# A prologue rebuilt: weights folded beside the first norm of a fused vision block

## The chip, the cores and the metric

The kernel runs on one core of a Trainium2 chip. The metric is the device time of one execution in microseconds (us), the median of several runs. The engines are TensorE (PE; its weight loads PEld), VectorE (DVE), ScalarE (ACT), GpSimd (POOL) and SyncE (SP); the last issues most of the DMA transfers, ACT issues a few at the start.

## The reference, cut to what matters

Four images are cut into patches and embedded; a class token goes ahead of them (3137 tokens of 128 features each). A gated delta attention and then a feed-forward block with mixed expert weights follow.

```python
emb = jnp.einsum('blk,ek->ble', patches, W) + b            # K = 48 pixels
x0  = jnp.concatenate([cls_tok, emb], axis=1)
xn  = _layernorm(x0)
q_c = _dwconv_causal(_linear(xn, Wq, bq), cwq, cbq)         # 4 taps; the same for k and v
...
outs = scan(gated delta rule over q, k, v with gates from Wa, Wb)
h1  = x0 + (gated, normalised outs) @ Wo.T + bo
y   = h1 + layernorm(hn + FFN(hn)), with FFN weights mixed by a gate of hn
```

(The snippet is shortened from the reference, whose parts are nested functions. `hn` is the normalised `h1`.)

## The kernel before, in words

The tokens go through in 25 steps of 128 tokens, each for the four images at once. A software pipeline of five stages runs over the steps: the body for index `j` does the embedding stage E of step `j+2`, the projections F of step `j+1`, the inner triangular solve I of step `j`, the state update C of step `j-1` and the output stage H of step `j-2`. The first body is `j = -2` (`first`) and has only stage E of step 0. Each engine runs its own program of these bodies in an order written out by hand, and semaphores tie the engines together; an engine runs its instructions strictly in that order. After the last body the feed-forward part begins, 25 units of it.

Because the embedding is linear, the kernel never forms q, k and v from the normalised tokens by two products. It folds, once, in the prologue: the embedding weights `We` (48 pixel rows, a bias row, an empty row and a class row, `KX` = 51 in all) are centred (`Wc`, the mean over the 128 features taken off), transposed (`WcT`), multiplied with all projections (`rhs_all`: k, v, gate, q and the two scalar gates, 514 columns) and, for k, v and q, multiplied with the four convolution taps. The taps are spread over partitions by small products with selection matrices (`selA`, `selB`, `cwT`), and the convolution's bias by one with `onehot1` and `cb_row`. The results are `SA` and `SB`. From then on a step's projections are products of `SA` and `SB` with `xs`, the pixel columns times the norm's reciprocal deviation.

That deviation takes a trip: stage E multiplies pixels and `We` (L1088), DVE takes the statistics (L810, L818), POOL the power -1/2 (L625, L628), PE transposes the four columns to rows (L1111), ACT copies them to SBUF (L479), SP writes them to HBM (L395), waits, and reads them back broadcast over partitions (L400, L401). DVE multiplies them with the pixels to `xs` (L911), ACT copies the shifted half (L528), and then PE may start the projections of the step (L1050, L1051), the first thing of the body `j = -1` on it.

In the body `j = -2` DVE runs `fold_weights` and `sub_masks` (L711 to L725) ahead of L911; PE runs its `fold_weights` at the very end of the body. All eight early weight loads share one semaphore, `w_in`, and the bias row `bo_rows` for the residual shares `we_in` with the embedding's weights. In `fold_weights` DVE makes every step wait for the one before (`step_done`). `apart(engine)` issues a no-operation between a wait and the next instruction.

The scalar program begins so:

```python
for s in (0, 1):
    act.dma_start(xt[s][0:KX], x[:, :, s * C:(s + 1) * C]).then_inc(xt_in[s], 16)
for dst, src in weights_early[1::2]:
    act.dma_start(dst, src).then_inc(w_in, 16)
```

## Time and profile before

| | before |
|---|---|
| median of 3 runs | 891.03 us (890.76 to 892.22) |
| profiled execution, its own time | 895.05 us |
| its span in the profile | 893.2 us |
| PE busy | 838.4 us (94%) |
| DVE busy | 664.9 us (74%) |
| ACT busy | 482.1 us (54%) |
| POOL busy | 355.4 us (40%) |

A span is what the profiler saw from the first to the last instruction; the execution's own time has 1.85 us more around it. Busy time counts matmuls from start to modelled end, and since they overlap in a pipeline a busy PE is not one at its peak. Times of rows are microseconds from the span's start.

### The profile page before, as it was taken

To read this page: it belongs to the slowest core of one execution; us is meant where nothing else is said; L and a number is where in the kernel's file an instruction comes from. 1 tells how busy PE (TensorE), PEld (TensorE's weight loads), DVE (VectorE), ACT (ScalarE), POOL (GpSimd) and SP (SyncE) were. 2 spreads that over 40 slices of the span, in tenths; PEclk is the share of its full clock that TensorE was granted. 3 is DMA by queue.
4 is the path that set the end of the run, shared out by engine and by line. 5 is a ranking of instruction groups with operands and counts; after the bars stand their busy time and mean duration, and the time that the engine had idled before them with its cause. 6 is when DMAs were issued, how large, how long until landed. Compare 5 with 4: busy or idle time off the path is not lost. (4 is left out here: it accounts for less than half of the span.)

```text
span 893.2 us, 31060 instructions
## 1 busy us (share of the span) xinstructions
PE 838.4 (94%) x11766; PEld 634.7 (71%) x11766; DVE 664.9 (74%) x2420; ACT 482.1 (54%) x1721; POOL 355.4 (40%) x530
## 2 busy tenths in 40 slices
PE   5689999999999999999999999999985999999996
PEld 2357777777777777777777777777764677777775
DVE  3466888888888888888888888888764676868434
ACT  0434455565655565565655565566523355666654
POOL 3122333233332332233332332333211178888875
PEclk9999999999999999999999999999958799999999
DMA  2000121222111110111110110111100233333431
GB/s 62 10 13 12 48 54 49 59 60 59 38 53 48 36 32 24 36 36 37 32 35 24 33 34 24 37 31 30 28 26 24 90 96 111 107 107 114 122 119 43
DMA packets 78659, 45.33 MB, mean 51 GB/s; under 512 B 20357, under 2 KB 69803, under 8 KB 78511
## 3 DMA queue, kind: packets, MB, share of 16 engines
q1 hardware_dynamic: 77663, 42.80, 16.8%
q8 instruction: 95, 1.56, 0.7%
q10 hardware_dynamic: 848, 0.54, 0.2%
q14 instruction: 53, 0.43, 0.2%
HBM read 23.69 MB, written 19.63 MB: 49 GB/s over the span
## 5 line engine op out<-in xcount | busy, mean ns | idle before, releaser
L1050 PE MATMUL bank<-SA,work 128*128 128x386 f32 x200 | 93.5, 550 | 6.5 <-ACT work L528 6.5
L1647 PEld LDWEIGHTS bank<-work 128*128 128x128 f32 x768 | 89.6, 192 | 12.5 <-issue 12.5
L1529 ACT ACTIVATE work<-bank,b1mix 128x512 f32<-128x512 f32 x96 | 66.0, 687 | 59.4 <-PE bank L1621 59.3
L438 ACT ACTIVATE logit<-bank 128x2 f32<-128x2 f32 x100 | 17.3, 173 | 149.3 <-PE bank L1051 149.1
L1647 PE MATMUL bank<-work 128*128 128x128 f32 x768 | 89.9, 275 | 0.8 <-DVE work L1407 0.8
L616 POOL TENSOR_SCALAR var2e<-mv 128x4 f32<-128x4 f32 x25 | 5.7, 227 | 211.1 <-DVE mv L795 211.1
L1621 PE MATMUL bank<-work 128*128 128x512 f32 x192 | 86.5, 593 | 0.0
L1051 PE MATMUL bank<-SB,work 128*128 128x256 f32 x200 | 60.8, 386 | 0.0
L1621 PEld LDWEIGHTS bank<-work 128*128 128x128 f32 x192 | 34.6, 190 | 34.6 <-issue 34.4
L1010 PEld LDWEIGHTS bank<-work 32*32 32x32 f32 x3200 | 35.6, 108 | 32.9 <-issue 27.2
L1051 PEld LDWEIGHTS bank<-SB,work 128*128 128x128 f32 x200 | 38.9, 194 | 27.9 <-issue 1.8
L1446 DVE TENSOR_TENSOR work<-bank,work 128x512 f32<-128x512 f32 x24 | 16.6, 691 | 56.1 <-PE bank L1647 56.1
L1010 PE MATMUL bank<-work 32*32 32x32 f32 x3200 | 46.1, 195 | 8.9 <-DVE work L950 8.0
L1038 PEld LDWEIGHTS bank<-work 32*32 32x32 f32 x3200 | 35.1, 108 | 26.6 <-issue 21.1
L639 POOL COPY work<-work 32x128 f32<-32x128 f32 x50 | 14.1, 282 | 94.9 <-DVE work L755 93.8
L1038 PE MATMUL bank<-work 32*32 32x32 f32 x3200 | 46.1, 195 | 4.0 <-DVE work L744 4.0
L753 DVE TENSOR_TENSOR work<-bank,work 128x128 f32<-128x128 f32 x100 | 28.6, 286 | 27.6 <-PE bank L1038 27.5
L486 ACT ACTIVATE work<-bank 128x128 f32<-128x128 f32 x100 | 26.2, 277 | 41.5 <-PE bank L1125 41.5
L441 ACT ACTIVATE work<-bank 128x384 f32<-128x384 f32 x100 | 48.5, 485 | 0.0
L744 DVE TENSOR_TENSOR work<-bank,masks 128x128 f32<-128x128 f32 x100 | 28.5, 285 | 26.5 <-PE bank L1010 26.3
L625 POOL TENSOR_SCALAR var1e<-mv 128x4 f32<-128x4 f32 x25 | 5.6, 224 | 100.5 <-DVE mv L818 100.5
L634 POOL TENSOR_TENSOR expo<-euler,logit 128x8 f32<-128x8 f32 x25 | 40.9, 1636 | 6.8 <-ACT logit L438 4.0
(233 smaller groups left out, 2287.8 us busy)
## 6 DMA issues: line engine op xcount, KB each, us to landing
hn_kept<-work SPq DMA_DIRECT2D x25, 256.0 KB, 2.3
hnT_kept<-work SPq DMA_DIRECT2D x25, 256.0 KB, 2.3
work<-hnT_kept SPq DMA_DIRECT2D x25, 256.0 KB, 2.9
work<-hn_kept SPq DMA_DIRECT2D x25, 256.0 KB, 3.1
out_dram<-work SPq DMA_DIRECT2D x24, 256.0 KB, 2.5
tv<-in_L_ffn_tv_W_dram SPq DMA_DIRECT2D x16, 256.0 KB
work<-r_kept SPq DMA_DIRECT2D x25, 98.0 KB
work<-in_x_dram SPq DMA_DIRECT2D x23, 102.0 KB
```

Source lines behind the costliest of these rows:

```text
L441: nc.scalar.activation(kvg[s % 3][:, b, :], bank[4 - b % 2][:, 0:384], ACT.Silu).then_inc(kvg_ready, 1)
L486: ins = nc.scalar.activation(sq_q[:, b, :], by4(bank[1])[:, b, :], ACT.Square, accum_out=ssq[:, b:b + 1])
L634: nc.gpsimd.tensor_tensor(expo[:, :], euler[:, :], logit[:, :], ALU.pow).then_inc(expo_ready, 1)
L744: nc.vector.tensor_tensor(newblk[k], by32(blk_ps), masks32[:, MASKED.index(k), :].unsqueeze(1).broadcast_to([D, NB, SUB]), ALU.mult).then_ ...
L753: nc.vector.tensor_tensor(Xd[par], by32(X_ps), Xd[par], ALU.add).then_inc(X_ready, 1)
L1010: ins = mm(by32(blk_ps)[sub(r), b], Bm[par][sub(r), b, sub(r)], Yd[par][sub(r), b, :], start=True, stop=True)
L1038: ins = mm(by32(X_ps)[sub(r), b], newblk[k][sub(r), b, :], Xd[par][sub(r), b, :], start=True, stop=True)
L1050: mm(t[:, 0:386], xs[p][:, b, HIST:XW], SA[:, 0:386], start=True, stop=False)
L1051: mm(t[:, 0:256], xs[p][:, b, 1:1 + C], SB[:, 0:256], start=False, stop=True).then_inc(kvg_ps, 1)
L1529: ins = nc.scalar.activation(hid[f][:, :], ps[:, :], ACT.Relu, bias=b1mix[:, of[0], f:f + 1])
L1621: ins = mm(ps[:, :], w1T[of[0]][:, f, :], ghT[par][:, :, :].rearrange("p t c -> p (t c)"), start=True, stop=True)
L1647: ins = mm(by4(bank[2 + par])[:, t, :], hid[f][:, t * C:(t + 1) * C], w2T[of[t]][:, f, :], start=(f == 0 and t == 0), stop=(f == FB - 1), ...
```

## The change

It touches the prologue above all. The weight loads get semaphores of their own: `taps_in` for the taps, `proj_in` for the projections and their biases, `bo_in` for the residual's bias row, `w_in` for what is needed later; they are issued in another order. PE first runs eight products of `ones` with itself whose result nobody reads (`WARM`), then the three products of taps and convolution bias, then stage E of step 0, and its `fold_weights` stands right behind that instead of at the end of the body, ahead of L1111. The product with the projections is cut into two parts, k, v and q first and the gates behind them, so 514 columns are made in four pieces instead of two. ACT keeps the three results of the taps in SBUF and the gate part of `SA`; it runs one Silu on ones before that. DVE centres the weights before the statistics, copies `WcT` right behind them, and multiplies the taps straight out of PSUM with six operations, with no copy to `fold`; the chain `step_done` is gone. `h` of step 0 is kept behind the copy of `WcT`. Elsewhere two `apart(dve)` of stage E go, and the last feed-forward unit counts on the semaphores of the other units instead of its own.

```diff
@@ -338,13 +347,12 @@
             return not isinstance(j, int) or 0 <= j + lag < STEPS
 
         first, last = -2, STEPS + 1
+        WARM = 8
 
         def iterations(body):
             for j in range(first, last + 1):
                 body(j, j % 2)
 
-        DVE_PRO = 16
-
         LE, LF, LI, LC, LH = 2, 1, 0, -1, -2
         TV_FROM = 2
         block = ctx.enter_context(nc.Block())
@@ -357,14 +365,13 @@
 
         embedding = [
             (We[0:PIX, :], tok_WT[:, :]), (We[PIX:PIX + 1, :], row1(tok_b)),
-            (We[PIX + 2:PIX + 3, :], tok_cls.rearrange("a b p -> (a b) p")), (bo_rows[:, :], bo.partition_broadcast(D)),
+            (We[PIX + 2:PIX + 3, :], tok_cls.rearrange("a b p -> (a b) p")),
         ]
-        weights_early = [
-            (cwT, taps_kvq[:, :]), (bias_row[:, 0:514], row1(biases[0:514])), (cb_row[:, 0:384], row1(biases[514:898])),
-            (rhs_all[:, 0:514], projections[:, :]), (nat[:, 0, :], WoT[:, :]), (nat[:, 1, :], gfc1_wT[:, :]),
-            (nw_col, col1(norm_w)), (gfc1_bc[:, :], col1(gfc1_b)),
-        ]
-        W_IN = 16 * len(weights_early)
+        conv_taps = [(cwT, taps_kvq[:, :]), (cb_row[:, 0:384], row1(biases[514:898]))]
+        projection = [(rhs_all[:, 0:514], projections[:, :]), (bias_row[:, 0:514], row1(biases[0:514]))]
+        later_sp = [(nat[:, 0, :], WoT[:, :]), (nw_col, col1(norm_w))]
+        later_act = [(nat[:, 1, :], gfc1_wT[:, :]), (gfc1_bc[:, :], col1(gfc1_b))]
+        W_IN = 16 * (len(later_sp) + len(later_act))
 
 
         ffn = make_ffn(nc, ctx, sb, sem, work, locals())
@@ -374,7 +381,10 @@
             sp.wait_ge(We_zero, 1)
             for dst, src in embedding:
                 sp.dma_start(dst, src).then_inc(we_in, 16)
-            for dst, src in weights_early[0::2]:
+            for dst, src in conv_taps:
+                sp.dma_start(dst, src).then_inc(taps_in, 16)
+            sp.dma_start(bo_rows[:, :], bo.partition_broadcast(D)).then_inc(bo_in, 16)
+            for dst, src in later_sp:
                 sp.dma_start(dst, src).then_inc(w_in, 16)
             ffn["load"](sp)
 
@@ -419,10 +429,21 @@
         @block.scalar
         def _(act):
 
-            for s in (0, 1):
-                act.dma_start(xt[s][0:KX], x[:, :, s * C:(s + 1) * C]).then_inc(xt_in[s], 16)
-            for dst, src in weights_early[1::2]:
+            act.dma_start(xt[0][0:KX], x[:, :, 0:C]).then_inc(xt_in[0], 16)
+            for dst, src in projection:
+                act.dma_start(dst, src).then_inc(proj_in, 16)
+            act.dma_start(xt[1][0:KX], x[:, :, C:2 * C]).then_inc(xt_in[1], 16)
+            for dst, src in later_act:
                 act.dma_start(dst, src).then_inc(w_in, 16)
+            act.wait_ge(ones_set, 1)
+            nc.scalar.activation(gate_sums[:, 0, :], ones[:, 0:NB], ACT.Silu)
+            act.wait_ge(taps_ps, 1)
+            for t, i in ((cwA, 0), (cwB, 4), (cbs, 2)):
+                ins = nc.scalar.copy(t, bank[i][:, 0:384])
+            ins.then_inc(taps_kept, 1)
+            act.wait_ge(gate_ps, 1)
+            nc.scalar.copy(SA[0:64, 256:386], bank[6][0:64, 0:130]).then_inc(gate_kept, 1)
+
             def body(j, par):
                 p = 1 - par
 
@@ -660,19 +681,12 @@
 
         @block.vector
         def _(dve):
-            done = [0]
-
-            def step_done(ins):
-
-                done[0] += 1
-                ins.then_inc(pro_dve, 1)
-                dve.wait_ge(pro_dve, done[0])
-
             nc.vector.memset(We[:, :], 0.0).then_inc(We_zero, 1)
             ffn["vector_early"](dve)
 
             nc.vector.memset(Wc, 0.0)
             nc.vector.memset(WcT, 0.0)
+            nc.vector.memset(SA[64:128, 256:386], 0.0)
             nc.vector.memset(xs[0], 0.0)
             nc.vector.memset(xs[1], 0.0)
             for t in X:
@@ -680,38 +694,42 @@
             nc.vector.memset(Y, 0.0)
             nc.vector.memset(state, 0.0).then_inc(zeroed, 1)
 
+            def center_weights():
+                dve.wait_ge(we_in, 16 * len(embedding))
+                dve.wait_ge(zeroed, 1)
+                nc.vector.tensor_reduce(wsum[0:KX, :], We[0:KX, :], AX.X, ALU.add).then_inc(pro_dve, 1)
+                dve.wait_ge(pro_dve, 1)
+                nc.vector.tensor_scalar(wmean[0:KX, :], wsum[0:KX, :], 1.0 / D, None, ALU.mult).then_inc(pro_dve, 1)
+                dve.wait_ge(pro_dve, 2)
+                nc.vector.tensor_scalar(Wc[0:KX, :], We[0:KX, :], wmean[0:KX, :], None, ALU.subtract).then_inc(Wc_ready, 1)
+
             def fold_weights():
+                dve.wait_ge(WcT_ps, 1)
+                nc.vector.tensor_copy(WcT.rearrange("p (h c) -> p h c", h=2)[:, :, 0:KX],
+                                      bank[3][:, 0:KX].unsqueeze(1).broadcast_to([D, 2, KX])).then_inc(WcT_ready, 1)
+
+            def fold_taps():
+                dve.wait_ge(fold_ps, 1)
+                dve.wait_ge(taps_kept, 1)
+                kv, q = bank[5][:, 0:256], bank[5][:, 256:384]
+                nc.vector.tensor_tensor(SA[:, 0:256], cwA[:, 0:256], kv, ALU.mult).then_inc(pro_dve, 1)
+                nc.vector.tensor_tensor(SA[:, 386:514], cwA[:, 256:384], q, ALU.mult).then_inc(pro_dve, 1)
+                dve.wait_ge(pro_dve, 3)
+                nc.vector.tensor_tensor(SA[:, 0:256], cbs[:, 0:256], SA[:, 0:256], ALU.add)
+                nc.vector.tensor_tensor(SB[:, 0:256], cwB[:, 0:256], kv, ALU.mult)
+                dve.wait_ge(pro_dve, 4)
+                nc.vector.tensor_tensor(SA[:, 386:514], cbs[:, 256:384], SA[:, 386:514], ALU.add)
+                nc.vector.tensor_tensor(SB[:, 384:512], cwB[:, 256:384], q, ALU.mult).then_inc(folded, 1)
+
+            def output_weights():
                 dve.wait_ge(con, 2)
-                dve.wait_ge(zeroed, 1)
-                step_done(nc.vector.tensor_reduce(ident32[:, :], ident[:, :].rearrange("p (r c) -> p c r", r=SUBS), AX.X, ALU.add))
+                nc.vector.tensor_reduce(ident32[:, :], ident[:, :].rearrange("p (r c) -> p c r", r=SUBS), AX.X, ALU.add).then_inc(pro_dve, 1)
+                dve.wait_ge(w_in, W_IN)
+                nc.vector.tensor_scalar(Wo_T[:, :], nat[:, 0, :], nw_col, None, ALU.mult)
+                nc.vector.tensor_copy(gfc1_T[:, :], nat[:, 1, :])
+                dve.wait_ge(pro_dve, 5)
                 for t in Xd:
                     nc.vector.tensor_copy(t, ident32[:, :].unsqueeze(1).broadcast_to([D, NB, SUB]))
-
-                dve.wait_ge(we_in, 16 * len(embedding))
-                dve.wait_ge(w_in, W_IN)
-                step_done(nc.vector.tensor_reduce(wsum[0:KX, :], We[0:KX, :], AX.X, ALU.add))
-                step_done(nc.vector.tensor_scalar(wmean[0:KX, :], wsum[0:KX, :], 1.0 / D, None, ALU.mult))
-                step_done(nc.vector.tensor_scalar(Wc[0:KX, :], We[0:KX, :], wmean[0:KX, :], None, ALU.subtract))
-                step_done(nc.vector.tensor_scalar(Wo_T[:, :], nat[:, 0, :], nw_col, None, ALU.mult))
-                step_done(nc.vector.tensor_copy(gfc1_T[:, :], nat[:, 1, :]))
-
-                dve.wait_ge(pro_pe, 1)
-                step_done(nc.vector.tensor_copy(WcT.rearrange("p (h c) -> p h c", h=2)[:, :, 0:KX],
-                                                bank[3][:, 0:KX].unsqueeze(1).broadcast_to([D, 2, KX])))
-                dve.wait_ge(pro_pe, 2)
-                step_done(nc.vector.tensor_copy(fold[:, 0:512], bank[5][:, :]))
-                step_done(nc.vector.tensor_copy(fold[:, 512:514], bank[6][:, 0:2]))
-                for dst, taps in ((SA, bank[0]), (SB, bank[4])):
-                    step_done(nc.vector.tensor_tensor(dst[:, 0:256], taps[:, 0:256], fold[:, 0:256], ALU.mult))
-                    dst_q = dst[:, 386:514] if dst is SA else dst[:, 384:512]
-                    step_done(nc.vector.tensor_tensor(dst_q, taps[:, 256:384], fold[:, 384:512], ALU.mult))
-                step_done(nc.vector.tensor_tensor(SA[:, 0:256], bank[2][:, 0:256], SA[:, 0:256], ALU.add))
-                step_done(nc.vector.tensor_tensor(SA[:, 386:514], bank[2][:, 256:384], SA[:, 386:514], ALU.add))
-
-                nc.vector.memset(SA[64:128, 256:386], 0.0)
-                nc.vector.tensor_copy(SA[0:64, 256:384], fold[0:64, 256:384])
-                step_done(nc.vector.tensor_copy(SA[0:64, 384:386], fold[0:64, 512:514]))
-                assert done[0] == DVE_PRO
 
             def sub_masks():
 
@@ -801,22 +819,34 @@
                     need(dve, vmean_ready, s)
                     nc.vector.tensor_reduce(vsum[:, :], kvg[s % 3][:, :, D:2 * D], AX.X, ALU.add).then_inc(vsum_ready, 1)
                 grow(2)
+                if j == first:
+                    center_weights()
                 if on(j, LE):
                     s = j + LE
+
+                    def keep_h0():
+                        if s == 0:
+                            dve.wait_ge(bo_in, 16)
+                        h = h1buf[:, :, bass.ds(s, 1), :].rearrange("p b s c -> p b (s c)")
+                        nc.vector.tensor_tensor(h, by4(bank[1]), bo_rows[:, :].unsqueeze(1).broadcast_to([D, NB, D]), ALU.add).then_inc(h0_kept, 1)
+
                     dve.wait_ge(h0_ps, s + 1)
                     need(dve, mv1_ready, s)
-                    apart(dve)
                     for b in range(NB):
                         ins = nc.vector.bn_stats(stats1[:, b, :], by4(bank[1])[:, b, :])
                     ins.then_inc(stats1_done, 1)
-                    h = h1buf[:, :, bass.ds(s, 1), :].rearrange("p b s c -> p b (s c)")
-                    nc.vector.tensor_tensor(h, by4(bank[1]), bo_rows[:, :].unsqueeze(1).broadcast_to([D, NB, D]), ALU.add).then_inc(h0_kept, 1)
+                    if s > 0:
+                        keep_h0()
                     dve.wait_ge(stats1_done, s + 1)
                     need(dve, var1e_ready, s)
-                    apart(dve)
                     for b in range(NB):
                         ins = nc.vector.bn_aggr(mv1[:, b, :], stats1[:, b, :])
                     ins.then_inc(mv1_ready, 1)
+                    if s == 0:
+                        fold_weights()
+                        keep_h0()
+                        fold_taps()
+                        output_weights()
                 new_blocks(3)
                 if on(j, LH):
                     s = j + LH
@@ -899,8 +929,7 @@
                     dve.wait_ge(rk2_ready, s + 1)
                     need(dve, cdecay_ready, s)
                     nc.vector.scalar_tensor_tensor(cneg[:, :], rk2[:, :], -1.0, ab[:, 4:8], ALU.mult, ALU.mult).then_inc(cneg_ready, 1)
-                if isinstance(j, int) and j == first:
-                    fold_weights()
+                if j == first:
                     sub_masks()
                 if on(j, LE):
                     s = j + LE
@@ -961,26 +990,30 @@
         def _(pe):
             mm = nc.tensor.matmul
             tr = nc.tensor.transpose
+            pe.wait_ge(ones_set, 1)
+            for i in range(WARM):
+                mm(bank[7][:, 0:D], ones[:, :], ones[:, :], start=True, stop=True)
             pe.wait_ge(con, 2)
+            pe.wait_ge(taps_in, 16 * len(conv_taps))
+            mm(bank[0][:, 0:384], selA, cwT, start=True, stop=True)
+            mm(bank[4][:, 0:384], selB, cwT, start=True, stop=True)
+            mm(bank[2][:, 0:384], onehot1, cb_row[:, 0:384], start=True, stop=True).then_inc(taps_ps, 1)
             pe.wait_ge(we_in, 16 * len(embedding))
-            pe.wait_ge(zeroed, 1)
 
             def fold_weights():
-                pe.wait_ge(w_in, W_IN)
-
-                mm(bank[0][:, 0:384], selA, cwT, start=True, stop=True)
-                mm(bank[4][:, 0:384], selB, cwT, start=True, stop=True)
-                mm(bank[2][:, 0:384], onehot1, cb_row[:, 0:384], start=True, stop=True)
-                pe.wait_ge(pro_dve, 4)
-                tr(bank[3][:, 0:D], Wc, ident[:, :]).then_inc(pro_pe, 1)
-                pe.wait_ge(pro_dve, 7)
-
-                mm(bank[5][:, :], WcT, rhs_all[:, 0:512], start=True, stop=False)
-                mm(bank[5][:, :], onehot2, bias_row[:, 0:512], start=False, stop=True)
-                mm(bank[6][:, 0:2], WcT, rhs_all[:, 512:514], start=True, stop=False)
-                mm(bank[6][:, 0:2], onehot2, bias_row[:, 512:514], start=False, stop=True).then_inc(pro_pe, 1)
-                pe.wait_ge(pro_dve, DVE_PRO)
-                pe.wait_ge(con, 2 + 2 * len(MASKED))
+                pe.wait_ge(zeroed, 1)
+                pe.wait_ge(Wc_ready, 1)
+                tr(bank[3][:, 0:D], Wc, ident[:, :]).then_inc(WcT_ps, 1)
+                pe.wait_ge(WcT_ready, 1)
+                pe.wait_ge(proj_in, 16 * len(projection))
+                for to, at, n in ((0, 0, 256), (256, 384, 128)):
+                    mm(bank[5][:, to:to + n], WcT, rhs_all[:, at:at + n], start=True, stop=False)
+                    ins = mm(bank[5][:, to:to + n], onehot2, bias_row[:, at:at + n], start=False, stop=True)
+                ins.then_inc(fold_ps, 1)
+                for to, at, n in ((0, 256, 128), (128, 512, 2)):
+                    mm(bank[6][:, to:to + n], WcT, rhs_all[:, at:at + n], start=True, stop=False)
+                    ins = mm(bank[6][:, to:to + n], onehot2, bias_row[:, at:at + n], start=False, stop=True)
+                ins.then_inc(gate_ps, 1)
 
             def body(j, par):
                 p = 1 - par
@@ -1087,6 +1120,8 @@
                     for b in range(NB):
                         ins = mm(by4(bank[1])[:, b, :], xt[par][0:KX, b, :], We[0:KX, :], start=True, stop=True)
                     ins.then_inc(h0_ps, 1)
+                if j == first:
+                    fold_weights()
                 level_update(2)
                 if F_:
                     pe.wait_ge(kvg_ready, NB * s1 + 1)
@@ -1173,8 +1208,10 @@
                         pe.wait_ge(og_ready, NB * c + b + 1)
                         ins = tr(by4(bank[7])[:, b, :], og[:, b, :], ident[:, :])
                     ins.then_inc(ogT_ps, 1)
-                if isinstance(j, int) and j == first:
-                    fold_weights()
+                if j == first:
+                    pe.wait_ge(taps_kept, 1)
+                    pe.wait_ge(folded, 1)
+                    pe.wait_ge(gate_kept, 1)
 
             iterations(body)
             ffn["tensor"](pe)
...
@@ -1466,25 +1497,25 @@
-                                    fhnb[par][:, ts, :], ALU.add).then_inc(last_res, 1)
-            dve.wait_ge(last_res, i + 1)
+                                    fhnb[par][:, ts, :], ALU.add).then_inc(res_ready, 1)
+            dve.wait_ge(res_ready, LASTU + i + 1)
...
```

## Rows read from the trace of the kernel before

**Rows 1.** Waits, all engines, 0 to 30 us: total, times, longest.

```profile
ACT work L528 <- DVE work L911: 15.5, 1, 15.5
```

**Rows 2.** Waits of PE, 130 to 680 us: total, times, longest.

```profile
PE bank L1010 <- DVE work L950: 4.0, 20, 0.2
```

**Rows 3.** Timeline of the start: start, duration, engine, line, operands, count, idle before.

```profile
0.79 0.20 POOL L552 MEMSET ones<- 128x128 f32 x1 [0.29 <-POOLq L1681]
...
2.30 0.37 SPq L376 DMA_DIRECT2D bo_rows<-in_L_attn_bo_dram  x1
...
3.08 0.52 SPq L378 DMA_DIRECT2D work<-in_biases_dram  x1
...
6.07 2.04 PE L1088 MATMUL bank<-We,work 51*128 51x128 f32 x8 [6.07 <-DMA bo_rows<-in_L_attn_bo_dram]
...
8.23 0.89 DVE L810 BATCH_NORM_STATS2 stats<-bank 128x6 f32<-128x128 f32 x4 [3.61 <-PE bank L1088]
...
9.63 0.37 DVE L818 BATCH_NORM_AGGREGATE mv<-stats 128x2 f32<-128x6 f32 x4
...
10.67 0.28 DVE L692 TENSOR_REDUCE work<-We 51x1 f32<-51x128 f32 x1
...
11.60 0.37 PE L1111 MATMUL bank<-ident,rstd 128*4 128x128 f32 x1 [3.49 <-POOL rstd L628]
...
12.29 0.25 SPq L395 DMA_DIRECT2D r_kept<-work  x1
...
13.77 0.26 SPq L401 DMA_DIRECT2D work<-r_kept  x1
```

**Rows 4.** Timeline of the fold, to the first projections.

```profile
11.90 1.64 PE L971 MATMUL bank<-work 4*128 4x384 f32 x2
...
16.04 0.47 PE L975 MATMUL bank<-ident,work 128*128 128x128 f32 x1
16.62 0.26 DVE L699 COPY work<-bank 128x102 f32<-128x102 f32 x1 [4.25 <-PE bank L975]
...
16.94 2.08 PE L978 MATMUL bank<-work 128*128 128x512 f32 x2 [0.42 <-DVE work L699]
...
20.95 0.59 PE L980 MATMUL bank<-work 128*128 128x2 f32 x2
...
23.07 0.42 DVE L705 TENSOR_TENSOR SA<-bank,work 128x256 f32<-128x256 f32 x1
...
25.09 0.29 DVE L709 TENSOR_TENSOR SA<-bank,SA 128x128 f32<-128x128 f32 x1
...
26.04 0.17 DVE L719 MEMSET masks<- 128x128 f32 x1
...
27.03 0.68 DVE L911 TENSOR_TENSOR work<-work 51x512 f32<-51x512 f32 x1
...
28.57 1.63 PE L1050 MATMUL bank<-SA,work 128*128 128x386 f32 x2 [6.53 <-ACT work L528]
```

**Rows 5.** Busy time of DVE in one short stretch: stretch, length, busy (count), PEclk, DMA.

```profile
11.45:12.40 0.95, 0.86 (x2) 1.00 0.00 0
```

**Rows 6.** Timeline, rows of the next body.

```profile
33.05 1.16 PE L1088 MATMUL bank<-We,work 51*128 51x128 f32 x8
...
40.74 0.26 SPq L401 DMA_DIRECT2D work<-r_kept  x1
...
42.36 1.06 PE L1159 MATMUL bank<-work 128*128 128x128 f32 x8
...
42.71 0.69 DVE L911 TENSOR_TENSOR work<-work 51x512 f32<-51x512 f32 x1
```

**Rows 7.** Busy time of PE and its granted clock (the column after the count).

```profile
28.00:33.00 5.00, 4.43 (x8) 1.00 0.08 21
46.50:47.00 0.50, 0.50 (x32) 0.57 0.08 26
49.50:50.00 0.50, 0.50 (x33) 0.51 0.00 0
```

43 lines of the change are left out of this document (23 added, 20 removed).

## Prediction

> **What bounds the kernel now.** I read the waits of PE in the steady part first: the largest comes once a step, 0.2 us behind the small transpose of DVE [rows 2]. PE and DVE pace the loop, and the change does nothing there. So its worth lies ahead of the first projections. The waits of the first 30 us show ACT waiting 15.5 us for the product that makes `xs` [rows 1]; the timeline says why. The norm's trip is early: L401 is issued at 13.77 us [rows 3], and the same transfer lets L911 run 1.97 us after its issue one step later (40.74 to 42.71, where DVE had ended its work 0.1 us before) [rows 6], so the row was there by 15.7. L911 starts only at 27.03, because DVE must first end `fold_weights` and `sub_masks` [rows 4]. The fold ends last, with 11.3 us of slack beside it. 1.54 us after L911 PE starts L1050 [rows 4]; everything later hangs on that start through semaphores alone, no timer and no late load, so I carry a shift of L911 to the end one to one.
>
> **A note on PE's clock.** The granted clock reads 1.00 over the first 33 us [rows 7], yet stage E's eight matmul records take 2.04 us at 6.07 and 1.16 at 33.05 [rows 3, 6]. By durations PE is on the low of its two levels (1.2 GHz) until about 33, then on the high one (2.4). Dense work began at 28.57 and the high rate was there 4.5 us later; it began near 46.5 and the clock rose at 50.0, 3.5 us later [rows 4, 6, 7]. Between 11.90 and 22 PE was nearly always busy and stayed low (L978 2.08 us) [rows 4], largely with products that use one or four rows. It fell at about 46.6, 3.1 us after its last dense work ended at 43.42 [rows 6, 7].
>
> **The change, part by part.** Let H be the end of stage E's product, 8.11 before.
>
> *Warm matmuls.* Stage E's four products took 2.04 us, 0.51 each [rows 3], so eight take 4.1 at the low rate, from 1.0 (`ones` is set then [rows 3]) to 5.1. They cost nothing while the taps are still on their way; without that cover, up to 4.1.
>
> *Loads.* The taps move ahead of `bo_rows`, so their last part is issued near 2.7 instead of 3.08 [rows 3]. Landing isn't shown. From L395 to L401 are 1.48 us with a small transfer's whole way in them, and `bo_rows`, issued at 2.30, released PE at 6.07, 3.8 later [rows 3]. By these the taps land between 4.2 and 6.5; I take 5.5, nearer to the neighbour in the same queue. The only hard upper bound is that `w_in` was full when L692 began at 10.67. The projections and the bias on ACT's queue are issued earlier than before and needed later than 11; free. `bo_in` is waited for behind the copy of `WcT`, past 10: free; were it late, the taps' six operations would queue behind it.
>
> *The taps' products first.* From L971 to L975 they took 4.14 us [rows 4]; they now stand ahead of stage E. At the low rate: 5.5 + 4.1 + 2.04, H = 11.7. At the high rate half of that, by the two times of stage E [rows 3, 6]: 5.5 + 2.2 + 1.16, H = 8.9. If the clock rises at the end of the warm matmuls and falls some 3 us later, near 8, the taps run mostly high (2.6) and stage E low: H = 10.1. That is what I take, since 4.1 us of dense work lies between the 3.5 and 4.5 that two rises took.
>
> *Beside the first norm.* The centring (L692 to L694, 0.78 from 10.67 to the stretch at 11.45 [rows 3, 5]) goes in front of the statistics, into DVE's wait. L813, the 0.5 between L810 and L818, goes behind [rows 3]. `WcT` is copied at H + 1.5 (0.12 + 0.89 + 0.37 and gaps) for 0.26; its transpose (0.47) hides under the statistics. PE folds from H + 1.85. Two passes of 512 columns take about 2.0 [rows 4]; k, v and q are 384 columns in two contributions: 3.0 at the low rate. The gates: 128 columns in two contributions, 1.0, and the two scalar columns twice 0.55 (L980) [rows 4], 2.1. So k, v, q end at H + 4.85, the gates at H + 6.95. The three copies of taps on ACT (some 0.6 each, by DVE's 0.42 for 256 columns [rows 4]) have the 4 us and more between the taps' end and that moment.
>
> *DVE behind the fold.* The six operations from L705 to L709 took 2.31 us (23.07 to 25.38) [rows 4]; the new six have the same shapes: H + 7.25. Gone are 1.0 for the copies to `fold` (L980 and its equal L981 end near 22.05, L705 starts at 23.07) and 0.66 for three small operations (25.38 to 26.04). `output_weights` takes the 0.7 between L818's end and L692 [rows 3] and the 0.86 of Wo and gfc1 [rows 5]: H + 8.9. `sub_masks`, 0.99 (26.04 to 27.03) [rows 4]: DVE is free at H + 9.9. POOL makes the masks that it waits for behind its power, from H + 3.0 on; they have 5.9 us, and no row shows how much of it they need.
>
> *The norm's trip is now behind the fold.* L1111 queues behind the gates' products on PE, and L479 behind `gate_kept` on ACT; the reciprocal deviation is ready at H + 3.0 (11.60 less 8.11, less the 0.5 of L813). From L1111 to SP's L395 are 0.69, to L401 another 1.48 [rows 3], to L911 1.97 [rows 6]: H + 6.95 + 4.15 = H + 11.1. It ends 1.2 after DVE. So the wait moves from the fold to the row's transfer, which had been hidden; if that landed 1.2 sooner, DVE would be next.
>
> The Trainium skill ("DMA: Bandwidth & Descriptors", Anatomy of one DMA) puts a fixed cost of about 2.0 us on every DMA, mostly the receipt. The first of the two transfers here needs less than that by the rows; an estimate by the page would make the trip some 0.8 longer.
>
> *Rest.* ACT's second table load goes with the early Silu; the two `apart` stand where DVE waits for PE anyway; the merged semaphores keep every wait. All nothing.
>
> **Sum.** L911 at 10.1 + 11.1 = 21.2 instead of 27.03: 5.8 us earlier. The profiled execution's 895.05 (span 893.2 and 1.85 around it) would be 889.2. It lies 4.0 above the median of the runs shown, so the shift is taken off that: 891.03 - 5.8 = 885.2. The clock's later rises may fall otherwise by one us either way; with the taps' landing that gives the forecast's own range, 884.0 to 886.4.
>
> **Rivals.**
> *The clock never rises in the prologue.* The second rise took 3.5 us, the first 4.5, so 4.1 may be too few; the low-row products behind did not lift it before. H = 11.7, L911 at 22.8, 4.2 gained: 886.8.
> *It stays high through the fold.* H = 8.9; k, v, q 1.5; the gates 1.05; DVE is free at H + 8.3 and the row there at H + 8.5. L911 at 17.4, 9.6 gained: 881.4. Against it: from 5.1 on PE has only thin products and gaps, and it fell 3.1 us after dense work ended. In between (high for stage E too) 7 gained: 884.0.
> The Trainium skill ("TensorE: Matmul & The Clock Gate", Part 1) states that the low rate is the default, that sustained activity lifts it and idleness drops it again. By that rule the first rival is a matter of how the eight matmuls fall in time, run by run, and the second unlikely. The trace agrees in both rises and the fall named above.
> *The taps land late.* PE is in order: stage E, once at 6.07, stands behind them. The only hard bound is 10.67. Landing then gives H = 10.6 + 4.1 + 2.04 = 16.7, L911 at 27.8: 0.8 slower, 891.8. It decides from a landing at 9.8. For it: `w_in`'s larger loads fill the same queues at that time. Against: the taps are a few KB ahead of them in the queue, and PE was released by the fourth load at 6.07.
> *The gain is given back.* If something later ran on its own clock (loads, the clock's phases), the end would stay: 891.0. Against it: the waits show none of that kind [rows 1, 2].
>
> **How the numbers follow.** Forecast 0.45, clock never up 0.22, higher clock for longer 0.2 (half of it within 884), taps late 0.06, given back 0.07. Faster, same, slower by 0.2% (1.8 us, about what a measurement can tell from no change): the first three cases give 0.87, the lost gain and half of the late taps fall within, 0.10, and the other half, with a landing still later than the old order's bound, gives 0.03. The range reaches down to 882.6, leaving out the fully high clock, and up to 887.8, past the clock that never rises with the taps a microsecond late.
>
> **What would show it.** Stage E's records ending near 10 and lasting 2.04 (or 1.16: then higher); the taps' products in 2.6; the product to `xs` starting near 21, DVE idle before it by about 1 us with a DMA as releaser; PE's first projections near 22.8; the distance from there to the span's end unchanged within 1.5 us. The forecast is wrong if stage E comes later than 12, if a load holds PE past 7, or if DVE, not the row, ends last.

## The result, and the profile after

The changed kernel takes 889.08 us (median of 20 runs, 886.18 to 892.96); the kernel before, run beside it, 892.56 (20 runs). The ratio is 0.9965, with a 95% interval of 0.9953 to 0.9977: 3.1 us faster, 2.1 to 4.2. The forecast was 885.2 with a range of 882.6 to 887.8 and a gain of 5.8 us, so the time lies above the range and the gain is 3.1 of the 5.8. 1.5 us of the miss in absolute time is the reference: the three runs shown before had a median of 891.03. The rest is a real shortfall.

The profiled execution took 890.64 us, its span is 888.8. PE in the prologue, to the first product that uses the finished row, by the timeline:

```profile
1.05 3.79 PE L995 MATMUL bank<-ones 128*128 128x128 f32 x16 [1.05 <-POOL ones L573]
6.42 1.61 PE L998 MATMUL bank<-work 4*128 4x384 f32 x2 [1.59 <-DMA work<-in_biases_dram]
...
10.52 2.07 PE L1121 MATMUL bank<-We,work 51*128 51x128 f32 x8
12.53 0.47 PE L1006 MATMUL bank<-ident,work 128*128 128x128 f32 x1
14.14 1.22 PE L1010 MATMUL bank<-work 128*128 128x256 f32 x2 [1.14 <-DVE work L708]
15.29 1.22 PE L1011 MATMUL bank<-work 1*128 1x256 f32 x2
16.43 0.80 PE L1010 MATMUL bank<-work 128*128 128x128 f32 x2
...
17.88 0.80 PE L1014 MATMUL bank<-work 128*128 128x128 f32 x2
...
19.33 0.59 PE L1014 MATMUL bank<-work 128*128 128x2 f32 x2
...
20.36 0.38 PE L1146 MATMUL bank<-ident,rstd 128*4 128x128 f32 x1
```

The warm matmuls (L995) are over at 4.84. PE then stands idle 1.6 us for the last load of the taps, at work from 6.42, and stage E (L1121) comes at 10.52 where it came at 6.07 before [rows 3]. It takes 2.07 us, against 2.04 before and 1.16 at the high clock [rows 6]: the clock has not risen. The transpose of the reciprocal deviation (L1146) stands behind all four pieces of the fold.

The same execution on the other engines:

```profile
12.63 0.89 DVE L836 BATCH_NORM_STATS2 stats<-bank 128x6 f32<-128x128 f32 x4 [6.27 <-PE bank L1121]
...
17.99 0.42 DVE L715 TENSOR_TENSOR SA<-work,bank 128x256 f32<-128x256 f32 x1 [3.31 <-PE bank L1011]
...
19.39 0.28 DVE L722 TENSOR_TENSOR SB<-work,bank 128x128 f32<-128x128 f32 x1
...
20.73 0.76 DVE L741 TENSOR_REDUCE masks<-masks 128x16 f32<-128x64 f32 x4
...
21.05 0.25 SPq L405 DMA_DIRECT2D r_kept<-work  x1
22.22 0.27 SPq L410 DMA_DIRECT2D work<-r_kept  x1
22.53 0.26 SPq L411 DMA_DIRECT2D work<-r_kept  x1
24.34 0.68 DVE L940 TENSOR_TENSOR work<-work 51x512 f32<-51x512 f32 x1 [2.85 <-issue]
```

DVE has ended everything else at 21.49 and idles 2.85 us ahead of L940, the product to `xs`. Its releaser is not shown, but between the read's issue at 22.53 and 24.34 nothing else is under way that L940 waits for: it is the row's transfer. L940 starts 2.69 us earlier than L911 did [rows 4].

From there on nothing has changed but the clock's phases. Starts of the product to `xs` of the first and the last step, of the sum over the gates (the first instruction of the feed-forward part on DVE), and the span, for the profiled execution of every kernel of this study whose profile is used:

```
kernel              first xs  last xs   gate sum  span    xs to xs  xs to sum  sum to end
before              27.03     618.11    696.56    893.2   591.08    78.45      196.64
changed             24.34     615.59    691.99    888.8   591.25    76.40      196.81
changed again       25.04     617.92    696.38    893.1   592.88    78.46      196.72
no warm             24.45     616.07    687.92    884.5   591.62    71.85      196.58
row first           22.15     616.64    690.43    887.3   594.49    73.79      196.87
norm first          18.41     610.32    686.25    883.0   591.91    75.93      196.75
... and no warm     19.67     611.06    686.94    883.5   591.39    75.88      196.56
... and warm 12     17.75     608.30    684.23    881.0   590.55    75.93      196.77
one product         23.34     614.63    691.03    887.8   591.29    76.40      196.77
masks early         17.73     609.00    684.89    881.7   591.27    75.89      196.81
tap loads first     19.93     613.08    689.01    885.9   593.15    75.93      196.89
changed, warm 12    22.93     613.86    692.36    889.0   590.93    78.50      196.64
best again          16.55     611.37    685.21    882.0   594.82    73.84      196.79
```

The feed-forward part is the same to 0.3 us. The loop differs by up to 4.3 us and the stretch from the last `xs` to the gate sum by up to 6.7, and much of that is chance between executions: the changed kernel and its repetition differ by 4.3 us in span with 0.7 of it at the first `xs`. So a single span says little here, the start of the first `xs` says what the prologue did, and the median of many runs says what it is worth. Where the 6.7 us come from the granted clock shows. For the changed kernel, then for the one with no warm matmuls, PE's busy time and granted clock (the column after the count):

```profile
650.00:660.00 10.00, 8.18 (x186) 0.56 0.09 29
...
680.00:690.00 10.00, 3.73 (x14) 0.64 0.13 42
690.00:700.00 10.00, 10.00 (x35) 0.50 0.36 118
```

```profile
650.00:660.00 10.00, 7.08 (x230) 1.00 0.10 30
...
680.00:690.00 10.00, 6.63 (x21) 0.51 0.38 116
```

In the pipeline's last bodies PE has gaps. In the first execution the clock is at its low level (1.2 GHz) for more than half of the 50 us from 650, in the second it stays high (2.4 GHz) until after 680. All thirteen profiles fall in line: over the stretch from the last `xs` to the gate sum the mean granted clock is 0.82 in the three that take 78.5 us, 0.85 in the seven that take 75.9 to 76.4, 0.89 in the two that take 73.8, and 0.95 in the one that takes 71.85. The 890.64 of the changed kernel's profile against the 895.05 before holds 2.7 us of the change and 1.7 of this kind.

### The profile page after: what moved, and what is told of

The parts are those of the page before. It is cut to its first block and busy times, and to the rows that moved or that the text cites. A ratio compares the mean times of both kernels' runs of the same rounds, so it can differ in the third digit from the quotient of the medians.

```text
span 888.8 us, 31105 instructions
## 1 busy us (share of the span) xinstructions
PE 841.8 (95%) x11790; PEld 639.4 (72%) x11790; DVE 663.8 (75%) x2416; ACT 482.7 (54%) x1725; POOL 356.1 (40%) x530
```

## The experiments

Except where it says otherwise each kernel is the changed kernel with the edit shown. Ratios are to the kernel before, run on the same chip, with their 95% interval.

**The changed kernel again.** 

> The changed kernel once more, unaltered, as the measure for the other runs of this chip. In its first profile the eight warm matmuls ran at the low clock to their end (3.79 us from 1.05), stage E ended at 12.59 us and the product to xs began at 24.34. Theory A (the warm matmuls rarely or never raise the clock): this profile shows the same three numbers within 0.3 us, and the time is 3 to 4 us below the kernel before. Rival B (they raise it in some executions): with luck this profile shows stage E in some 1.2 us instead of 2.07 and the product to xs before 22.5; the median is the same, since it mixes both.

No edit. Median 888.56 us (12 runs), ratio 0.9962 (0.9946 to 0.9979). The low clock again (3.79 us for the warm matmuls, 2.07 for stage E); the taps landed later, at 6.80, and `xs` started at 25.04, 0.7 later than in the first profile, of which 0.4 is the landing and 0.3 the row's read. That is outside the 0.3 of theory A; for the clock theory A stands by this one profile, but it can't tell how often the clock rises.

**No warm matmuls.** 

> The changed kernel with none of the eight warm matmuls. Theory A (they do nothing but run under the taps' loads): the taps' products start at 6.4 as before, stage E ends at 12.6, the product to xs starts at 24.3, and the time equals the changed kernel's within 0.5 us. Rival B (in some executions they raise the clock, which is where the 0.8 us of median gain beyond the 2.7 us of the profile's prologue come from): the median is 0.8 to 1.5 us above the changed kernel's.

```diff
-        WARM = 8
+        WARM = 0
```

Median 889.78 us, ratio 0.9962 (0.9944 to 0.998): the same ratio as with the eight. The taps' products start at 6.50, `xs` at 24.45. The eight have cost nothing, and no gain of theirs can be told in the time.

**The row's transpose ahead of the gates.** 

> The changed kernel, but the transpose of the reciprocal deviation stands on PE between the products of k, v, q and those of the gates, and ACT copies the row before the gate columns. Theory A (the row's trip behind the gates' products is now what ends last): the row starts at 18.0 instead of 20.4, its trip of 4.0 us ends at 22.0, DVE is free at 21.5; the product to xs starts near 22.0, 2.3 us earlier, and the time falls by 2.3. Rival B (DVE's chain or the later bodies take it back): the product to xs moves by less than 0.5 us, or it moves and the end does not.

```diff
                 ins.then_inc(fold_ps, 1)
+
+            def fold_gates():
                 for to, at, n in ((0, 256, 128), (128, 512, 2)):
...
                     tr(bank[7][0:NB, 0:C], rstd1[:, :], ident[:, :]).then_inc(r_row_ps, 1)
+                if j == first:
+                    fold_gates()
...
-            act.wait_ge(gate_ps, 1)
-            nc.scalar.copy(SA[0:64, 256:386], bank[6][0:64, 0:130]).then_inc(gate_kept, 1)
...
                     nc.scalar.copy(rrows[64:64 + NB, 0, :], bank[7][0:NB, 0:C]).then_inc(r_row_ready, 1)
+                    if s == 0:
+                        act.wait_ge(gate_ps, 1)
+                        nc.scalar.copy(SA[0:64, 256:386], bank[6][0:64, 0:130]).then_inc(gate_kept, 1)
```

`xs` starts at 22.15, 2.2 us earlier than in the changed kernel's profile. The median is 885.52, 3.0 below the changed kernel on the same chip, the ratio 0.9943 (0.9921 to 0.9965); the two intervals overlap, so the move of `xs` is the better evidence. The row and DVE are now nearly level:

```profile
20.32 0.26 SPq L411 DMA_DIRECT2D work<-r_kept  x1
...
21.00 0.76 DVE L742 TENSOR_REDUCE masks<-masks 128x16 f32<-128x64 f32 x4
22.15 0.68 DVE L941 TENSOR_TENSOR work<-work 51x512 f32<-51x512 f32 x1 [0.40 <-DVE masks L742]
```

DVE's idle time has shrunk from 2.85 us to 0.40, and 1.83 us again lie between the read's issue and `xs`. The row's trip behind the gates' products was what ended last in the changed kernel; here it and DVE's chain end within half a microsecond.

**Stage E ahead of the taps' products.** 

> As the run before it, and besides the taps' products stand behind stage E and the transpose of the centred weights instead of ahead of them, and the row's transpose ahead of the products of k, v, q. Theory A (the wait for the taps' loads, then their 4.1 us, delays stage E and the whole fold): stage E starts at 5.5 to 6.1 instead of 10.5, the taps run under DVE's statistics and the power, k, v, q start near 12.6 instead of 14.1, the row lands by 17, and DVE's chain ends last near 20.2: 4.1 us earlier than the changed kernel, 6.8 before the kernel before. Rival B (the order of the two does not matter, since PE has the same sum of work before the fold): the product to xs starts no earlier than in the run before it, near 22.0.

Beside the edit of the run before (the transposes of the later steps stay where they were; the guards for that are left out here):

```diff
             pe.wait_ge(con, 2)
-            pe.wait_ge(taps_in, 16 * len(conv_taps))
-            mm(bank[0][:, 0:384], selA, cwT, start=True, stop=True)
-            mm(bank[4][:, 0:384], selB, cwT, start=True, stop=True)
-            mm(bank[2][:, 0:384], onehot1, cb_row[:, 0:384], start=True, stop=True).then_inc(taps_ps, 1)
             pe.wait_ge(we_in, 16 * len(embedding))
...
                 tr(bank[3][:, 0:D], Wc, ident[:, :]).then_inc(WcT_ps, 1)
+                pe.wait_ge(taps_in, 16 * len(conv_taps))
+                mm(bank[0][:, 0:384], selA, cwT, start=True, stop=True)
+                mm(bank[4][:, 0:384], selB, cwT, start=True, stop=True)
+                mm(bank[2][:, 0:384], onehot1, cb_row[:, 0:384], start=True, stop=True).then_inc(taps_ps, 1)
+                pe.wait_ge(rstd1_ready, 1)
+                tr(bank[7][0:NB, 0:C], rstd1[:, :], ident[:, :]).then_inc(r_row_ps, 1)
                 pe.wait_ge(WcT_ready, 1)
```

Median 884.79 us, ratio 0.9919 (0.989 to 0.9948). `xs` starts at 18.41, 1.8 us earlier than expected. In this execution eight warm matmuls did raise the clock (stage E 1.13 us, the first of the taps' products 1.13 for 1.64 [rows 4]). The clock is taken out by the next run; without it `xs` is still 0.5 us ahead of the expectation.

**That, without warm matmuls.** 

> The kernel that puts stage E and the row's transpose ahead (the run of that name: product to xs at 18.41 us, stage E in 1.13 us at the high clock) without the eight warm matmuls. Theory A (its gain is mostly the order; the clock that rose in that one execution gave it stage E and one pass of the taps' products at the high rate): stage E takes 2.04 us from 6.1, the product to xs starts 1.3 to 1.6 us later, at 19.7 to 20.0. Rival B (the order is worth little and the raised clock made most of it): the product to xs starts after 21.5.

```diff
-        WARM = 8
+        WARM = 0
```

Median 885.13 us, ratio 0.9908 (0.9887 to 0.9928). Stage E takes 2.04 us from 5.77, and `xs` starts at 19.67: 1.3 us later than with the raised clock and 4.7 earlier than in the changed kernel. The order is worth these 4.7, 2.2 of them the row's place and 2.5 stage E's (good to 0.3, since the taps landed 0.3 us later in the profile that gives the split). The raised clock is worth 1.3, which the two ratios are too wide to show.

**That, with twelve.** 

> The same kernel with twelve warm matmuls, 5.7 us at the low clock, up to 6.7. Theory A (eight are too few in most executions, twelve are enough in nearly all): this profile shows stage E in some 1.15 us and the product to xs at 18.4 to 19.0; if the clock rises the twelve end before 6.1 and cost nothing. Rival B (no number of matmuls on constants raises it reliably): stage E takes 2.04 us and starts at 6.7, the product to xs at 20.5, and the time is 0.5 us above the run with none.

```diff
-        WARM = 8
+        WARM = 12
```

```profile
1.05 5.23 PE L996 MATMUL bank<-ones 128*128 128x128 f32 x24 [1.05 <-POOL ones L574]
6.21 1.16 PE L1126 MATMUL bank<-We,work 51*128 51x128 f32 x8
...
8.31 0.80 PE L1006 MATMUL bank<-work 4*128 4x384 f32 x2
8.95 1.15 PE L1007 MATMUL bank<-work 1*128 1x384 f32 x2
```

At the low rate a further record of this shape adds 0.21 us, so 24 would take 5.49 by the 3.79 for 16; they took 5.23, so the clock rose among the last of them. Stage E is short, a pass of the taps' products costs 0.80 a pair, and the last pair spans the fall. `xs` starts at 17.75, earlier than the 18.4 to 19.0 expected. Median 882.98 us, ratio 0.989 (0.9871 to 0.9909).

**One product instead of the cut one.** 

> The changed kernel with the product of weights and projections in the two pieces of the kernel before (512 and 2 columns) instead of four; the gate columns are copied by ACT only when DVE has ended the fold, since both sit in one PSUM bank. Theory A (each piece costs a fixed 0.3 us per contribution beside its columns, so the cut costs 1.1 us on the path that ends last, the row's trip behind the gates): the products end 5.1 us after they start instead of 6.2, and the product to xs starts 1.1 earlier, near 23.2, although the fold on DVE starts 0.3 later. Rival B (the extra is not the cut but the bank or the rows of the operands): the products take 6.2 us again and the product to xs stays at 24.3.

```diff
-                for to, at, n in ((0, 0, 256), (256, 384, 128)):
...
+                mm(bank[5][:, :], WcT, rhs_all[:, 0:512], start=True, stop=False)
+                mm(bank[5][:, :], onehot2, bias_row[:, 0:512], start=False, stop=True).then_inc(fold_ps, 1)
-                for to, at, n in ((0, 256, 128), (128, 512, 2)):
+                for to, at, n in ((0, 512, 2),):
```

ACT copies the row first, then waits for DVE's `folded` and copies the gate columns from the two banks; DVE reads q at columns 384 to 512.

```profile
14.29 2.07 PE L1012 MATMUL bank<-work 128*128 128x512 f32 x2 [1.13 <-DVE work L711]
16.29 2.07 PE L1013 MATMUL bank<-work 1*128 1x512 f32 x2
18.29 0.59 PE L1015 MATMUL bank<-work 128*128 128x2 f32 x2
...
19.33 0.37 PE L1147 MATMUL bank<-ident,rstd 128*4 128x128 f32 x1
```

From the first product to the row's transpose 5.04 us instead of 6.22, and `xs` starts at 23.34, 1.0 us earlier. Median 889.85 us, ratio 0.9956 (0.9936 to 0.9975); the time alone would not tell it from the changed kernel. A pair of records costs 2.0 us for 512 columns, 1.15 for 256 and 0.73 for 128: between these 0.3 us and 3.3 ns a column (a pair of 2 columns costs 0.52). The cut buys DVE 0.25 us of start and costs the row 1.2.

**Output weights and masks before the fold.** 

> The kernel with stage E ahead (eight warm matmuls), and besides DVE makes the output weights and the small masks while it waits for the products of k, v, q, ahead of the fold with the taps. Theory A (DVE's chain ends last there: it was idle 5.6 us before the fold and then did 1.9 us of work that nothing in the fold needs): the product to xs starts when the fold ends and the row has landed, 1.7 us earlier than in that run, 16.7 with a raised clock and 18.2 without; 8 to 10 us below the kernel before. Rival B (POOL's masks are late, or the row's trip is the next bound within 0.5 us): it moves by less than 0.7 us.

Added to the kernel with stage E ahead, with eight warm matmuls (`sub_masks` leaves its old place, and the counts waited for on `pro_dve` follow the new order):

```diff
-                        fold_taps()
                         output_weights()
+                        sub_masks()
+                        fold_taps()
```

Median 883.64 us, ratio 0.9895 (0.9875 to 0.9916). The clock had not risen in the profile. `xs` starts at 17.73, 1.9 us earlier than at the same clock with no warm matmuls. PE's first projections came 1.86 us behind it, where it had been 1.5: ACT copies the gate columns in between.

**All of it.** 

> All that helped so far: stage E and the row's transpose ahead, output weights and masks made while DVE waits, and twelve warm matmuls. Theory A (each removes its own piece): stage E in 1.16 us from 6.2, the fold on DVE from 14.2, the product to xs near 15.9 to 16.0, the first projections near 17.8, 10 to 11 us ahead of the kernel before, and the median 10 us below it. Rival B (the copy of the gate columns on ACT, behind the gates' products, holds the shifted copy of xs and PE): the first projections start later than 18.2 although the product to xs is at 16.

Added to the kernel of the run before:

```diff
-        WARM = 8
+        WARM = 12
```

One of its five executions, the profiled one, took 1570 us. The median of the five is 882.64 us, of the other four 882.59, and the ratio of these 0.9876 (0.9853 to 0.9899). In the profile of the long one PE alone is slow: it is busy for 1540.9 us, by 841.3 in the repetition below, while DVE is busy for 671.9, by 663.6. A record of 386 columns (L1087) takes 930 ns on average, where in the repetition it takes 899 while the clock is low and 540 in the middle of the loop. Why PE ran at no more than its low rate all through isn't known. The kernel was therefore run once more.

**The taps' loads issued first.** 

> The changed kernel with the two loads of taps and convolution bias issued ahead of the three of the embedding instead of behind them, so the second is issued at 1.5 us instead of 2.6. Theory A (a load lands some 3.8 us behind its issue and the taps' landing at 6.4 starts the whole chain): the taps' products start near 5.3, stage E ends near 11.5, the product to xs starts 1.1 us earlier, near 23.2. Rival B (they land by how full the queues are, not by when they are issued, or the embedding's weights become late): they start after 6.0 and the product to xs moves by less than 0.4 us.

```diff
+            for dst, src in conv_taps:
+                sp.dma_start(dst, src).then_inc(taps_in, 16)
             for dst, src in embedding:
                 sp.dma_start(dst, src).then_inc(we_in, 16)
-            for dst, src in conv_taps:
-                sp.dma_start(dst, src).then_inc(taps_in, 16)
```

```profile
1.05 3.58 PE L995 MATMUL bank<-ones 128*128 128x128 f32 x16 [1.05 <-POOL ones L573]
...
1.51 0.23 SPq L383 DMA_DIRECT2D work<-in_biases_dram  x1
...
4.71 0.91 PE L998 MATMUL bank<-work 4*128 4x384 f32 x2
...
6.84 1.33 PE L1121 MATMUL bank<-We,work 51*128 51x128 f32 x8
...
19.93 0.68 DVE L940 TENSOR_TENSOR work<-work 51x512 f32<-51x512 f32 x1 [2.87 <-issue]
```

The taps' products follow the warm matmuls without an idle time, so the load issued at 1.51 was there by 4.71, within 3.2 us; issued at 2.61 it had been there at 6.42. The clock had risen here too, so the 4.4 us at `xs` are not all the loads': 1.7 by the earlier start, 2.0 by the taps' products (2.1 us instead of 4.1), 0.7 by stage E. The earlier start is worth more than the 1.1 expected. It could not come much sooner, since POOL finishes the last of the selection matrices (L598) at 4.65. Median 887.12 us, ratio 0.9931 (0.991 to 0.9953).

**The changed kernel with twelve.** 

> The changed kernel with twelve warm matmuls instead of eight. Theory A (the prediction's central case, a raised clock that falls some 3 us later, was right in its mechanism and failed since eight matmuls do not raise the clock): the taps' products take 2.7 to 2.9 us instead of 4.1, stage E ends near 11.3 instead of 12.6, and the product to xs starts near 23.0. Rival B (the thin products of the taps are no faster at the raised clock, or it falls before them): they take 4.1 us and the product to xs stays within 0.3 us of 24.3.

```diff
-        WARM = 8
+        WARM = 12
```

```profile
1.05 4.71 PE L995 MATMUL bank<-ones 128*128 128x128 f32 x24 [1.05 <-POOL ones L573]
6.47 0.88 PE L998 MATMUL bank<-work 4*128 4x384 f32 x2 [0.71 <-DMA work<-in_biases_dram]
7.19 0.80 PE L999 MATMUL bank<-work 4*128 4x384 f32 x2
7.84 1.12 PE L1000 MATMUL bank<-work 1*128 1x384 f32 x2
8.89 2.07 PE L1121 MATMUL bank<-We,work 51*128 51x128 f32 x8
```

This is the case that the prediction took for the likeliest: the taps at the raised clock (2.4 us), the fall ahead of stage E, stage E low. It ends at 10.96 and `xs` starts at 22.93, by 23.0 expected. The 24 records took 4.71 us, 0.8 less than the 5.49 of the low rate. Median 887.54 us, ratio 0.9933 (0.9908 to 0.9957), whose interval overlaps that of the changed kernel.

**All of it, again.** 

> The kernel with all that helped, unaltered, for a profile of a usual execution. Theory A: as expected of it before, stage E in 1.16 us from 6.2, the product to xs near 16.0, the median 10 us below the kernel before. Rival B (ACT's copy of the gate columns, which waits for the gates' products on PE to end near 16.7, holds the shifted copy of xs that stands behind it): the product to xs starts near 16.0 but the first projections start 1.9 us behind it instead of 1.5.

No edit to the kernel with all of it. Median 882.07 us, ratio 0.9872 (0.9854 to 0.989): 11.4 us below the kernel before, the fastest of the study. On DVE, ACT and PE:

```profile
1.05 5.49 PE L995 MATMUL bank<-ones 128*128 128x128 f32 x24 [1.05 <-POOL ones L574]
6.46 1.44 PE L1125 MATMUL bank<-We,work 51*128 51x128 f32 x8
...
10.96 0.37 PE L1008 MATMUL bank<-ident,rstd 128*4 128x128 f32 x1 [0.67 <-POOL rstd L650]
...
16.55 0.68 DVE L940 TENSOR_TENSOR work<-work 51x512 f32<-51x512 f32 x1
16.74 0.58 PE L1019 MATMUL bank<-work 1*128 1x2 f32 x2
17.25 0.90 SPq L395 DMA_DIRECT2D work<-in_x_dram  x1
17.37 0.26 ACT L501 COPY SA<-bank 64x130 f32<-64x130 f32 x1 [5.51 <-PE bank L1019]
17.65 0.62 ACT L550 COPY work<-work 51x520 f32<-51x520 f32 x1
18.42 1.62 PE L1087 MATMUL bank<-SA,work 128*128 128x386 f32 x2 [1.09 <-ACT work L550]
```

`xs` starts 0.5 us later than expected. The twelve took 5.49 us, the low rate to their end, and the clock rose only among stage E's records, which took 1.44 us, between the 1.16 of the high and the 2.07 of the low clock; stage E so ended 0.5 us later than in the run with twelve above (7.90 and 7.37). Rival B is right beside theory A: the copy of the gate columns waits for the gates' products, the shifted copy of `xs` (L550) stands behind it, and the first projections start 1.87 us after `xs`. Besides, PE idles 0.67 us ahead of the row's transpose (L1008) for POOL's power, with the products of k, v, q queued behind. Neither was tried.

Set side by side, the gain at the first `xs` of the one profile (27.03 less its start) and the gain by the ratio (of some 893.5 us):

| kernel | gain at `xs`, us | gain by the ratio, us |
|---|---|---|
| changed | 2.7 | 3.1 |
| changed again | 2.0 | 3.4 |
| no warm | 2.6 | 3.4 |
| row first | 4.9 | 5.1 |
| norm first | 8.6 | 7.2 |
| norm first, no warm | 7.4 | 8.2 |
| norm first, twelve | 9.3 | 9.8 |
| one product | 3.7 | 3.9 |
| masks early | 9.3 | 9.4 |
| tap loads first | 7.1 | 6.2 |
| changed, twelve | 4.1 | 6.0 |
| best again | 10.5 | 11.4 |

They run together within 2 us, about the uncertainty of the ratios.

## Why the prediction was wrong, point by point

**What bounds the kernel.** Right. The prologue's chain to `xs` goes one to one into the time, within the 2 us that can be told, by all the kernels set side by side above. The two `apart` and the merged semaphores were priced at nothing and not tried alone; the loop (591.08 and 591.25 us from first to last `xs`) and the feed-forward part (196.64 and 196.81) give them no room.

**Warm matmuls.** The step that failed: "That is what I take", the clock that rises at the end of the warm matmuls, and with it H = 10.1 (H is the end of stage E's product). The clock stayed low and H was 12.59. Of seven used profiles with eight warm matmuls (changed, again, row first, norm first, one product, masks early, tap loads first) the clock rose in two, so the first rival, 4.2 us gained, was the likelier case. What a raised clock does was priced rightly: with twelve, in the changed kernel, the central case came out as described (stage E's end at 10.96, `xs` at 22.93). Whether it rises in time was luck. With twelve it rose in all three profiles, but by the records' durations some eight records before their end in one (4.71 us, which is about where eight matmuls end), among the last few in another (5.23), and behind their end in the third (5.49). So eight fell short, and twelve are not sure either. The prediction gave the wrong one of the two cases more than double the other's chance, from two rises that took 3.5 and 4.5 us of dense work, with 4.1 in hand (3.79 as it turned out, less than that).
The Trainium skill ("TensorE: Matmul & The Clock Gate", Part 1) warns that the point of the rise varies from run to run of one kernel. The traces agree: after eight warm matmuls the clock stayed low in five executions and rose in two, and after twelve it rose at three different points.

**Loads of the taps.** 5.5 was taken, 6.42 came, at the upper end of the 4.2 to 6.5 named, and 6.80 in the repetition, past it. 0.9 us. The nearer neighbour was `bo_rows` with 3.8 from issue to use; the taps' last load took the same 3.8 (2.61 to 6.42), and 4.2 in the repetition. The small write of the row was no measure for a read at the start.

**The taps' products first.** 4.1 at the low rate, right. That they stand ahead of stage E was priced, and seen as the change's cost; the runs with the order turned show that cost at some 2.5 us of `xs`.

**The fold.** Priced by columns, 5.1 us for k, v, q and gates; it took 6.2. A pair of records has a fixed share of 0.3 us beside its columns, and the change makes eight pairs out of four. The run with one product gave back 1.0 at `xs`. This is the second step that failed.

**DVE.** Six operations were to take 2.31 and took 1.68. Each is about as long as before (0.42 and 0.28 us, by 0.42 and 0.29), though one side now comes from SBUF; what is gone are the waits of each for its neighbour, so they overlap. DVE was free at H + 8.9, by H + 9.9 expected.

**The row's trip as the new end.** Right: L1146 to L940 took 3.98, against 4.14, with DVE idle before; the 1.97 taken for the read was an upper bound, since DVE had been at work until 0.1 us before, and the read took 1.81. `xs` came at H + 11.75 instead of H + 11.1, the excess from the fold.

**The sum.** Forecast for `xs` 21.2, measured 24.34. Landing 0.9, the taps at the low clock 1.5, the fold 1.1, the trip -0.2 and an earlier start of the fold behind H -0.3 (H + 1.55 for 1.85) make 3.0 of the 3.1. The first rival's 4.2 had the landing and the fold just as short; less 0.9 for the landing and 0.65 for H + 11.75 it gives the 2.7 of the profile, which lies in the interval of the measured gain, 2.1 to 4.2.

**The other rivals.** The clock high to the end of the fold occurred nowhere. Late taps and a gain given back did not occur either.

## What to carry to other kernels

When a chain is moved off the critical place, list what each engine's queue now holds ahead of the runner-up: here the norm's trip over HBM had 11 us of slack, and it became the end since its transpose was queued behind products that only the gates need. Start the step with the longest latency first (stage E, then the row), and put work with no reader nearby into the waits: this order with the same work gave 8.2 us where the change gave 3. Do not count on filler that should raise PE's clock: eight matmuls, with a length between the shortest and the longest rise seen, did nothing in five of seven profiles, and twelve, a whole microsecond longer than the longest, still ended ahead of the rise in one of three. Where it runs under a wait it costs nothing; its gain belongs in the sum with its chance, not whole.

## What the runs showed of the hardware

After the warm matmuls had raised the clock it fell again within microseconds, although PE was nearly always at work. For the changed kernel with twelve, the norm first with twelve and the best again, PE's busy time and granted clock (after the count):

```profile
8.00:8.50 0.50, 0.50 (x2) 0.69 0.86 60
```

```profile
9.00:9.50 0.50, 0.50 (x3) 0.78 0.57 184
```

```profile
10.00:10.50 0.50, 0.29 (x1) 0.99 1.17 321
```

The level goes from 1.00 to 0.50 within each stretch, so it fell at 8.2, 9.3 and 10.5, which is 2.4, 3.0 and 4.0 us behind the end of the warm matmuls (5.76, 6.28, 6.54). In the first two that is within the last pair of the taps' products, in the third just behind it. In the two profiles in which eight had raised it, the granted clock fell at 7.7 and 7.95, 3.0 and 3.2 us behind their end. Between the warm matmuls and the fall ran the taps' products of one and four rows and, in all but the changed kernel with twelve, stage E; products of these few rows had not raised the clock in the kernel before either, but no run here separates the rows from the rest. They do run faster while it is high: 0.80 us a pair against 1.48.

Where an engine waited for a load of the very start, 3.3 to 4.2 us lie between its issue and its use (at most 3.2 for the taps when issued first), while the row's write, later and alone, took 1.17 to the next issue and its read 1.8 to 2.1. The Trainium skill ("DMA: Bandwidth & Descriptors", Anatomy of one DMA) has about 2.0 us fixed for a transfer, in a section on those that GpSimd issues; these are SyncE's. The trace agrees for the read, is below it for the write and well above it for the first loads.

Executions of one kernel differ by 6.8 us in the changed kernel's twenty and by 12 in the twelve with one product. Between the profiles up to 6.7 us go with how long the clock is low in the last bodies, as shown above. With gains of 3 us that needs medians of a dozen runs, or a place in the profile ahead of the chance.
